# Two attentions, two feed-forwards: when scores may begin, and how far maxima run ahead

## The chip, the cores and the metric

The kernel runs on one core of a Trainium2 chip, which has eight. The metric is device time in microseconds of one execution, the median of several. Five engines take part: TensorE (PE; matmuls, and PEld, its weight loads), VectorE (DVE), ScalarE (ACT), GpSimd (POOL) and SyncE (SP), which here only issues DMAs. Each runs its own list of instructions in order and waits on semaphores for the others.

## The reference

Input x is 8 batches of 512 rows of 128 channels. Four layers follow one another, each with a residual and a layernorm behind it:

```python
x = L0_attn_x
x = _layernorm(x + _L0_attn_ref(x, Wqkv, Wproj))        # causal, rotary, 16 heads of 8
x = _layernorm(x + _L0_ffn_ref(x, ...))                  # 7 routed experts, top 2, one shared
x = _layernorm(x + _L1_attn_ref(x, Wq, Wk, Wv))          # the same without mask and projection
x = _layernorm(x + _L1_ffn_ref(x, ...))                  # gated, then three dense layers
```

The attention, which alone is changed, is

```python
Q = _apply_rope(Q, cos, sin); K = _apply_rope(K, cos, sin)
scores = einsum('bhqd,bhkd->bhqk', Q, K) / sqrt(8)
scores = where(causal, scores, finfo.min)                # layer 0 only
attn = softmax(scores)
y = einsum('bhqk,bhkd->bhqd', attn, V)
```

## The kernel before, in words

`attention` is written once and called twice, first causal (a0_), later without mask (a1_). Heads go in groups of four (HG = 4), so a batch has NG = 4 groups and all batches have 32. A group n takes PH phases: three if causal, four if not. Phase p belongs to group p // PH. A causal phase has one of three kinds: blocks of 512 columns; of 384 and 128; of 256. A batch is 12 phases (16 without mask), 96 in all (128). "Phase 5 of a batch" counts within the batch. Each phase has two halves of two heads.

Softmax needs each row's maximum, and it is taken ahead. `maxima(m, k)` computes the scores of phase m turned round, a head at a time, into one of three PSUM banks (ps_m, MB = 3); VectorE's `reduce_head` reduces each to a column of mx. When a group's maxima are known, GpSimd's `split_max` splits the negated values into two bf16 parts (L385, L387), TensorE's `turn_maxima` transposes them (L646), ScalarE copies them to mrow (L513), and SP's `max_rows` sends them by four DMAs into two more rows of qst (L325). Only then can `scores(p, half)` (L715) of that group run, which subtract the maximum in the matmul itself. ScalarE's `exp` follows (L537), GpSimd's `hide` sets the causal corner to zero (L396), and two phases later `weigh` multiplies by the values (L733).

The scores share two double banks (ps_s, SB = 2) with all other jobs of TensorE that ScalarE copies out: turn_x (L604), heads (L621), values (L628), stack (L639 and L640), turn_maxima, turn_y. They take the two banks in turn, in the order in which the planning code at the top of `attention` numbers them (S_AT). So a job waits for ScalarE's copy of the job two before it. M_AT does the same for ps_m.

A batch's way in: turn_x transposes x, heads makes q and k of all heads (copied to raw), SP's `swap_neighbours` makes a copy with pairs swapped (L333), four `rope_step`s for k and four for q rotate and split them into hi and lo (L363, L367, L373, L375; on VectorE for batch 0, on GpSimd for others), and `stack(b, i, half)` spreads them into kst (i = 0) or qst (i = 1) for the two groups of that half. Batch 0 does this ahead of the loop; batch 1's turn_x, heads and rotation stand ahead of the loop too, and later batches' are jobs at fixed phases of the loop (AT_STACK, AT_V, AT_XT, AT_HEADS, F_ROPE). The first maxima of a group with even number wait for ScalarE's copy of the stack that holds it.

LOOK is by how many phases maxima run ahead of scores: LOOK = PH + 3, so 6 if causal and 7 if not. All engines' lists are written out from the same tables; there is no scheduler.

Ahead of the loop TensorE runs:

```python
for m in range(LOOK):
    for k in range(HG):
        maxima(m, k)
    if m < 2: stack(0, m, 1)
    if m == 2: turn_x(1)
    if m == 3: heads(1)
    if m == PH: turn_maxima(0)
```

## Time and profile before

| | us |
|---|---|
| median of 3 runs | 1426.3 |
| lowest, highest | 1419.05, 1452.39 |
| the profiled execution | 1425.7 |
| its span | 1424.0 |
| TensorE busy | 1215.5 (85%) |
| VectorE, ScalarE, GpSimd busy | 849.9, 796.6, 620.8 |

The span is what the profiler saw from the first instruction to the last; the execution's own time is 1.7 us longer. The first attention lies between about 10 and 460 us of it, the second between about 684 and 1125. The granted clock in the profile's lines is a share of 2.4 GHz: 1.00 is that level, 0.50 is 1.2 GHz, and what lies between is a mixture over the stretch.

### The profile page before, as it was taken

The numbers are of one execution on the slowest core, as the hardware profiler recorded it, in microseconds if no ns is written. First come the engines' busy times: TensorE is split into PE (matmuls) and PEld (weight loads), VectorE is DVE, ScalarE is ACT, GpSimd is POOL, SyncE is SP. The second block draws the span as 40 slices with busy tenths as digits, with TensorE's granted clock in tenths as the row PEclk, the third lists the DMA queues.
The fourth block names the chain that finished last, engine by engine and source line by source line (L and its number), as shares of the span: only waits on it lengthen the run. The fifth ranks groups of instructions, "written<-read, shape, count | busy, mean of one in ns | idle before, by whom it ended". The sixth has DMA issues, their size and how long they took to land. (4 is left out here: it accounts for less than half of the span.)

```text
span 1424.0 us, 23092 instructions
## 1 busy us (share of the span) xinstructions
PE 1215.5 (85%) x8067; PEld 691.5 (49%) x8067; DVE 849.9 (60%) x2446; ACT 796.6 (56%) x1093; POOL 620.8 (44%) x790
## 2 busy tenths in 40 slices
PE   5688888888889497895589999999999779999996
PEld 2334434444444355773233444444434258888885
DVE  4466566656673467445558888888889032455443
ACT  2365556545554252543347877777878445555553
POOL 2454465655534567564133414523420325454552
PEclk8588778868776599998559999999999679999998
DMA  5000000000000000533030000000000000000000
GB/s 179 16 18 17 3 18 24 24 3 25 10 3 16 15 1 6 151 66 70 0 98 17 18 17 3 17 17 3 17 3 3 1 16 8 15 15 15 29 8 15
DMA packets 45847, 35.61 MB, mean 25 GB/s; under 512 B 5601, under 2 KB 37345, under 8 KB 45745
## 3 DMA queue, kind: packets, MB, share of 16 engines
q1 hardware_dynamic: 41760, 31.02, 6.9%
q0 software_dynamic: 3696, 2.76, 1.4%
q8 instruction: 58, 0.95, 0.3%
q10 hardware_dynamic: 288, 0.52, 0.1%
q14 instruction: 45, 0.36, 0.1%
HBM read 15.74 MB, written 8.06 MB: 17 GB/s over the span
## 5 line engine op out<-in xcount | busy, mean ns | idle before, releaser
L537 ACT ACTIVATE a_prob<-a_ps_s 128x1024 f32<-128x1024 f32 (+1 forms) x448 | 423.0, 964 | 140.3 <-PE a_ps_s L715 137.2
L807 DVE TENSOR_REDUCE a_mx<-a_ps_m 128x1 f32<-128x512 f32 x512 | 317.8, 682 | 73.5 <-PE a_ps_m L701 72.9
L701 PE MATMUL a_ps_m<-a_kst,a_qst 24*128 24x512 f32 (+3 forms) x1024 | 297.7, 498 | 19.0 <-DVE a_mx L803 11.3
L733 PE MATMUL a_ps_o<-a_prob,a_vst 128*32 128x256 f32 (+2 forms) x3328 | 302.5, 441 | 10.0 <-ACT a_oT L544 9.7
L803 DVE CUSTOM_DVE_ANT_0 a_junk<-a_ps_m,mask 128x128 f32<-128x128 f32 (+3 forms) x512 | 222.5, 486 | 130.1 <-PE a_ps_m L701 130.0
L715 PE MATMUL a_ps_s<-a_qst,a_kst 26*128 26x512 f32 (+3 forms) x1024 | 238.4, 484 | 39.8 <-ACT a_prob L537 20.6
L715 PEld LDWEIGHTS a_ps_s<-a_qst,a_kst 26*128 26x128 f32 x1024 | 100.8, 205 | 214.9 <-issue 108.7
L701 PEld LDWEIGHTS a_ps_m<-a_kst,a_qst 24*128 24x128 f32 x1024 | 137.3, 206 | 51.0 <-DVE a_mx L803 21.3
L396 POOL TENSOR_SCALAR_AFFINE_SELECT a_prob<-a_prob 128x512 f32<-128x512 f32 x128 | 79.9, 636 | 185.1 <-ACT a_prob L537 141.7
L1850 POOL TENSOR_TENSOR f_hid_lo<-f_gelu_h,f_hid_hi 128x512 fp32r<-128x512 f32 x64 | 83.1, 1298 | 101.3 <-ACT f_hid_hi L1813 101.3
L733 PEld LDWEIGHTS a_ps_o<-a_prob,a_vst 128*32 128x32 f32 x3328 | 70.9, 114 | 115.4 <-issue 99.0
L385 POOL TENSOR_SCALAR a_mpart<-a_mx 128x16 bf16<-128x16 f32 x64 | 16.5, 257 | 223.4 <-DVE a_mx L807 202.3
L1888 PE MATMUL f_ps_h<-f_hid_hi,f_h_hi 128*128 128x512 f32 x256 | 102.9, 402 | 4.0 <-POOL f_hid_lo L1850 4.0
L1890 PE MATMUL f_ps_h<-f_hid_lo,f_h_hi 128*128 128x512 f32 x256 | 101.5, 397 | 0.0
L1889 PE MATMUL f_ps_h<-f_hid_hi,f_h_lo 128*128 128x512 f32 x256 | 101.0, 395 | 0.0
L363 POOL TENSOR_TENSOR a_raw<-a_raw,rope_tables 128x1024 f32<-128x1024 f32 x28 | 66.6, 2377 | 34.2 <-DMA a_raw<-a_raw 33.1
L639 PE MATMUL a_ps_s<-a_hi,select 128*128 128x512 f32 x128 | 67.6, 528 | 12.4 <-POOL a_lo L375 6.3
L504 ACT ACTIVATE a_kst<-a_ps_s,unit 128x1024 fp32r<-128x1024 f32 x32 | 35.7, 1115 | 51.9 <-PE a_ps_s L640 51.9
L1850 POOL TENSOR_TENSOR f_hid_lo<-f_gated_h,f_hid_hi 128x512 fp32r<-128x512 f32 x32 | 41.5, 1296 | 46.7 <-ACT f_hid_hi L1802 46.0
L640 PE MATMUL a_ps_s<-a_lo,select 128*128 128x512 f32 x128 | 59.1, 462 | 0.0
L1244 ACT ACTIVATE f_gatea<-f_ps_a 128x512 f32<-128x512 f32 (+1 forms) x60 | 32.8, 547 | 44.9 <-PE f_ps_b L1338 37.3
L1888 PEld LDWEIGHTS f_ps_h<-f_hid_hi,f_h_hi 128*128 128x128 f32 x256 | 48.6, 190 | 16.2 <-POOL f_hid_lo L1850 6.5
(310 smaller groups left out, 2001.4 us busy)
## 6 DMA issues: line engine op xcount, KB each, us to landing
a_raw<-a_raw SPq DMA_DIRECT2D x28, 256.0 KB, 2.5
ef_w<-in_L_ffn_W_dram SPq DMA_DIRECT2D x21, 256.0 KB
a_qst<-a_mrow SPq DMA_DIRECT2D x256, 4.0 KB
x_tiles<-in_L_attn_x_dram SPq DMA_DIRECT2D x8, 256.0 KB, 4.6
normed_rows_dram<-ef_nrm SPq DMA_DIRECT2D x8, 256.0 KB, 2.3
f_sums<-expert_sums_dram SPq DMA_DIRECT2D x4, 512.0 KB, 5.3
f1w_h<-in_L_ffn_h_w_dram SPq DMA_DIRECT2D x2, 1024.0 KB, 6.9
f_xin<-x_tiles SPq DMA_DIRECT2D x8, 256.0 KB, 2.3
```

What stands on the lines that cost most here:

```text
L396: ins = pool.affine_select(out=diag, in_=diag, compare_op=ALU.is_ge, fill=0.0, base=0, pattern=[[0, HG], [1, P]], channel_multiplier=-1)
L537: act.activation(prob[p % RING][:, h:h + 2, 0:w], ps_s[S_AT["exp", p, u] % SB][:, :, 0:w], ACT.Exp, scale=float(D) ** -0.5).then_inc(s_tak ...
L639: pe.matmul(tile[:, v, :], select[:, i, 0, g, :], hi[:, i, :], start=True, stop=False)
L701: last = pe.matmul(tile[:, c0:c0 + w], qst[r][rows(hh, KEYS), g, P * i:P * i + P], kst[r][rows(hh, KEYS), g, 0:w], start=True, stop=True)
L715: last = pe.matmul(tile[:, v, c0:c0 + w], kst[r][rows(hh, SHIFTED), g, P * j:P * j + P], qst[r][rows(hh, SHIFTED), g, q0:q0 + w], start=Tr ...
L733: last = pe.matmul(ps_o[VW * hh:VW * hh + VW, q0:q0 + w], vst[b % 2][:, j, H // 2 * (g % 2) + HG * (g // 2) + hh, :], prob[p % RING][:, hh ...
L803: ins = dve.tensor_tensor_reduce(junk[M_AT["max", m, k] % 4][:, c0:c0 + w], tile[:, c0:c0 + w], mask[:, T - w:T], op0=ALU.add, op1=ALU.max ...
L807: ins = dve.reduce_max(mx[:, n % 2, h, i:i + 1], tile[:, c0:c0 + w], AX.X)
L1850: pool.tensor_tensor(dst, src[:, :], hi.bitcast(F32), ALU.subtract).then_inc(s_lo, 1)
L1888: pe.matmul(out, w_hi[w][:, k, cols], hi, start=start, stop=False)
L1889: pe.matmul(out, w_lo[w][:, k, cols], hi, start=False, stop=False)
L1890: return pe.matmul(out, w_hi[w][:, k, cols], lo, start=False, stop=stop)
```

## The change

Maxima ahead of the loop are cut from LOOK phases to FIRST = PH + 1. The missing ones are caught up in the loop: `known(p)` says how many phases' maxima have been issued by the end of phase p, and rises by two a phase until it reaches p + LOOK + 1. LOOK itself becomes seven if causal. Batch 0's second-half stacks move into phase 0. turn_maxima(0) now stands ahead of turn_x(1) and heads(1), and on SP max_rows(0) ahead of swap_neighbours(1). The transposes of group 1's maxima come a phase later (phase 1, or 2 without mask). Batch 1's rotation on GpSimd is dealt out over phases 0 to 3, two steps to each, behind `hide`. In every batch the next batch's first stacks move from phases 0 and 1, first half, to 3 and 4, second half; the causal second pair's q stack moves from phase 10 to 9 (without mask it stays at 12).

```diff
-    LOOK = PH + 3
+    LOOK = PH + (4 if causal else 3)
...
+    FIRST = PH + 1
...
-        AT_STACK = {(0, 0): (0, 0), (1, 0): (1, 0), (0, 1): (6, 0), (1, 1): (10, 0)}
+        AT_STACK = {(0, 0): (3, 1), (1, 0): (4, 1), (0, 1): (6, 0), (1, 1): (9, 0)}
...
-        AT_STACK = {(0, 0): (0, 0), (1, 0): (1, 0), (0, 1): (7, 0), (1, 1): (12, 0)}
+        AT_STACK = {(0, 0): (3, 1), (1, 0): (4, 1), (0, 1): (7, 0), (1, 1): (12, 0)}
...
     def turned_maxima(p):
 
+        if p in (PH - 3, PH - 2):
+            return 1 if p == PH - 2 else None
         n, now = divmod(p + 3, PH)
         return n if now == 0 and 0 < n < G else None
 
+    def known(p):
+
+        return min(PHASES, p + LOOK + 1, FIRST + 2 * (p + 1))
+
+    def maxima_at(p):
+
+        return range(known(p - 1), known(p))
...
     def stacked(p, u):
 
+        if p == 0:
+            return 0, u, 1
...
+                max_rows(0)
                 swap_neighbours(1)
-                max_rows(0)
...
                 split_max(0)
-                for i in range(2):
-                    for step in range(ROPE_STEPS):
-                        rope_step(pool, 1, i, step)
...
                     if causal and p < PHASES:
                         hide(p)
+                    if p < ROPE_STEPS:
+                        for step in (p % 2 * 2, p % 2 * 2 + 1):
+                            rope_step(pool, 1, p // 2, step)
...
-                for m in range(LOOK):
+                for m in range(FIRST):
                     for k in range(HG):
                         maxima(m, k)
-                    if m < 2:
-                        stack(0, m, 1)
-                    if m == 2:
-                        turn_x(1)
-                    if m == 3:
-                        heads(1)
-                    if m == PH:
-                        turn_maxima(0)
+                turn_maxima(0)
+                turn_x(1)
+                heads(1)
...
                         if live:
                             scores(p, half)
-                        if ahead_max:
-                            maxima(p + LOOK, 2 * half)
-                            maxima(p + LOOK, 2 * half + 1)
+                        for m in maxima_at(p):
+                            maxima(m, 2 * half)
+                            maxima(m, 2 * half + 1)
```

In the changed file the helpers' lines lie a few further on (L715 is L727, L701 is L713, L639 and L640 are L651 and L652, L646 is L658).

TensorE's list where the loop of attention 1 begins, before, from the last maxima of group 0 on. L701 is maxima, L604 turn_x, L621 heads, L646 turn_maxima, L715 scores; "x4" is the four heads.

```order
L701 MATMUL a_ps_m<-a_kst,a_qst 128x256 x4
L604 MATMUL a_ps_s<-ident,x_tiles 128x128 x4
L701 MATMUL a_ps_m<-a_kst,a_qst 128x512 x4
L621 MATMUL a_ps_s<-a_xT,heads_k 128x512
L621 MATMUL a_ps_s<-a_xT,heads_q 128x512
L646 MATMUL a_ps_s<-identb,a_mpart 32x128
L701 MATMUL a_ps_m<-a_kst,a_qst 128x128
L701 MATMUL a_ps_m<-a_kst,a_qst 128x384
```

Three more such pairs, four blocks of 256 and then L715 follow. The same place in the changed kernel:

```order
L713 MATMUL a_ps_m<-a_kst,a_qst 128x256 x4
L713 MATMUL a_ps_m<-a_kst,a_qst 128x512 x4
L658 MATMUL a_ps_s<-identb,a_mpart 32x128
L616 MATMUL a_ps_s<-ident,x_tiles 128x128 x4
L633 MATMUL a_ps_s<-a_xT,heads_k 128x512
L633 MATMUL a_ps_s<-a_xT,heads_q 128x512
L727 MATMUL a_ps_s<-a_qst,a_kst 128x512 x2
L713 MATMUL a_ps_m<-a_kst,a_qst 128x128
```

The transpose of the maxima stands ahead of turn_x and heads, and the scores follow the heads at once, with the maxima of phase 4 behind them.

TensorE's list in the changed kernel from the second half of phase 4 into phase 5 of the first batch, with its waits: a0_taken counts ScalarE's copies, a0_mtaken VectorE's, a0_rope1 the rotation of q. L651 and L652 are the q stack, L727 scores, L713 maxima of the next batch.

```order
L713 MATMUL a_ps_m<-a_kst,a_qst 128x256 [waits a0_mtaken] x2
L651 MATMUL a_ps_s<-a_hi,select 128x512 [waits a0_rope1,a0_taken]
L652 MATMUL a_ps_s<-a_lo,select 128x512
L651 MATMUL a_ps_s<-a_hi,select 128x512
L652 MATMUL a_ps_s<-a_lo,select 128x512
L727 MATMUL a_ps_s<-a_qst,a_kst 128x256 [waits a0_taken]
L727 MATMUL a_ps_s<-a_qst,a_kst 128x256
L713 MATMUL a_ps_m<-a_kst,a_qst 128x512 [waits a0_taken,a0_mtaken]
L713 MATMUL a_ps_m<-a_kst,a_qst 128x512 [waits a0_mtaken]
```

Before, nothing stood between phase 4's last maxima and phase 5's first scores, and phase 5 held the previous kind of maxima, still of the same batch. Now the stack stands there, and the first L713 behind it waits for ScalarE's copy of that very stack.

GpSimd's list at the start of attention 1, before: the split of group 0 (L385, L387), then all eight steps of batch 1's rotation, group 1's split, and only then `hide` (L396).

```order
L387 TENSOR_TENSOR a_mpart<-a_mx,a_mpart 128x4x4
L363 TENSOR_TENSOR a_raw<-a_raw,rope_tables 128x1024
L367 TENSOR_TENSOR a_rope<-a_raw 128x512
L373 CAST a_hi<-a_rope 128x512
L375 TENSOR_TENSOR a_lo<-a_rope,a_hi 128x512
...
L385 TENSOR_SCALAR a_mpart<-a_mx 128x4x4
L387 TENSOR_TENSOR a_mpart<-a_mx,a_mpart 128x4x4
L396 AFFINE_SELECT a_prob<-a_prob 128x4x128 x4
```

In the changed kernel:

```order
L400 TENSOR_TENSOR a_mpart<-a_mx,a_mpart 128x4x4
L409 AFFINE_SELECT a_prob<-a_prob 128x4x128
L376 TENSOR_TENSOR a_raw<-a_raw,rope_tables 128x1024
L380 TENSOR_TENSOR a_rope<-a_raw 128x512
L398 TENSOR_SCALAR a_mpart<-a_mx 128x4x4
L400 TENSOR_TENSOR a_mpart<-a_mx,a_mpart 128x4x4
L409 AFFINE_SELECT a_prob<-a_prob 128x4x128 x2
L386 CAST a_hi<-a_rope 128x512
L388 TENSOR_TENSOR a_lo<-a_rope,a_hi 128x512
```

The first `hide` and group 1's split no longer stand behind the whole rotation.

## Rows read from the trace of the kernel before

**Rows 1.** The page, busy time, share of the span and instructions of each engine.

```profile
PE 1215.5 (85%) x8067; PEld 691.5 (49%) x8067; DVE 849.9 (60%) x2446; ACT 796.6 (56%) x1093; POOL 620.8 (44%) x790
```

**Rows 2.** Windows: stretch, length, busy (count) of PE, PEld, DVE, ACT, POOL, clock.

```profile
26.05:70.12 44.07, 31.58 (x115) 16.41 (x116) 20.61 (x95) 11.80 (x16) 13.69 (x15) 0.50 0.08 26
698.74:742.47 43.73, 34.83 (x103) 16.57 (x104) 24.34 (x40) 13.85 (x17) 11.88 (x12) 0.50 0.26 79
70.00:460.00 390.00, 336.81 (x2634) 161.22 (x2634) 240.74 (x1110) 219.03 (x301) 200.94 (x330) 0.78 0.04 14
900.00:1000.00 100.00, 94.64 (x860) 40.90 (x857) 84.91 (x158) 79.13 (x94) 38.61 (x54) 1.00 0.04 15
```

**Rows 3.** Timeline, start of attention 1: start, duration, engine, line, tiles [idle before, releaser].

```profile
41.78 1.92 PE L621 MATMUL a_ps_s<-a_xT,heads_q 128*128 128x512 f32 x2
...
44.74 0.25 ACT L513 ACTIVATE a_mrow<-a_ps_s 32x128 f32<-32x128 bf16 x1
...
46.41 2.80 SPq L325 DMA_DIRECT2D a_qst<-a_mrow  x4
...
50.47 0.79 PE L715 MATMUL a_ps_s<-a_qst,a_kst 26*128 26x512 f32 x2 [1.86 <-DMA a_qst<-a_mrow]
```

**Rows 4.** Timeline, start of attention 1: reductions, a stack's matmul, a stack's copy.

```profile
28.11 0.69 DVE L803 CUSTOM_DVE_ANT_0 a_junk<-a_ps_m,mask 128x512 f32<-128x512 f32 x1
...
28.94 0.63 PE L640 MATMUL a_ps_s<-a_lo,select 128*128 128x512 f32 x1
...
30.46 1.11 ACT L504 ACTIVATE a_kst<-a_ps_s,unit 128x1024 fp32r<-128x1024 f32 x1 [4.47 <-PE a_ps_s L640]
...
31.51 0.55 DVE L803 CUSTOM_DVE_ANT_0 a_junk<-a_ps_m,mask 128x384 f32<-128x384 f32 x1
...
35.92 0.42 DVE L803 CUSTOM_DVE_ANT_0 a_junk<-a_ps_m,mask 128x256 f32<-128x256 f32 x1
```

**Rows 5.** Timeline, start of attention 2.

```profile
699.57 2.48 DVE L807 TENSOR_REDUCE a_mx<-a_ps_m 128x1 f32<-128x512 f32 x4 [4.13 <-PE a_ps_m L701]
...
719.59 1.28 ACT L537 ACT_TABLE_LOAD   x1
719.66 2.69 SPq L325 DMA_DIRECT2D a_qst<-a_mrow  x4
...
723.61 0.80 PE L715 MATMUL a_ps_s<-a_qst,a_kst 26*128 26x512 f32 x2
```

**Rows 6.** Timeline, attention 1, phases 0 and 1: TensorE behind GpSimd.

```profile
54.14 0.76 PE L639 MATMUL a_ps_s<-a_hi,select 128*128 128x512 f32 x1 [2.75 <-POOL a_lo L375]
...
60.48 0.27 PE L646 MATMUL a_ps_s<-identb,a_mpart 128*32 128x128 bf16 x1 [3.57 <-POOL a_mpart L387]
```

**Rows 7.** Two windows in the loop of attention 1, columns as in rows 2.

```profile
124.00:134.00 10.00, 8.43 (x87) 4.53 (x89) 6.19 (x26) 6.88 (x10) 6.05 (x8) 1.00 0.15 55
186.00:196.00 10.00, 9.12 (x64) 3.66 (x64) 8.82 (x47) 4.65 (x6) 5.31 (x8) 0.50 0.01 2
```

**Rows 8.** Waits of TensorE, 70 to 460: total us, times, longest.

```profile
PE a_ps_s L646 <- POOL a_mpart L387: 13.9, 10, 2.7
PE a_ps_m L701 <- DVE a_mx L803: 7.5, 9, 1.1
PE a_ps_s L715 <- ACT a_qst L506: 7.0, 13, 0.6
PE a_ps_s L715 <- ACT a_raw L485: 4.2, 6, 0.7
```

**Rows 9.** Windows: phase 9 at full and low clock, phases 10 and 11.

```profile
93.79:96.63 2.84, 2.70 (x26) 0.96 (x26) 2.70 (x10) 2.09 (x3) 2.25 (x3) 1.00 0.00 0
96.63:102.17 5.54, 4.92 (x52) 2.49 (x52) 4.78 (x25) 4.28 (x6) 3.03 (x4) 1.00 0.02 6
140.81:144.89 4.08, 3.63 (x26) 1.13 (x26) 3.11 (x10) 2.10 (x3) 1.61 (x3) 0.50 0.00 0
```

**Rows 10.** Timeline, phase 6 of the third batch: the transpose of maxima.

```profile
184.63 0.22 PE L646 MATMUL a_ps_s<-identb,a_mpart 128*32 128x128 bf16 x1 [1.67 <-POOL a_mpart L387]
```

More of the change, by code:

```diff
@@ L212, in m_slot @@
         M_AT[key] = len(M_AT)
-    for b in range(2):
-        s_slot("xT", b)
-        for i in range(2 if b == 0 else 1):
-            s_slot("heads", b, i)
-        if b == 0:
-            s_slot("v", 0)
-            for half in range(2):
-                for i in range(2):
-                    s_slot("stack", 0, i, half)
+    s_slot("xT", 0)
+    for i in range(2):
+        s_slot("heads", 0, i)
+    s_slot("v", 0)
+    for i in range(2):
+        s_slot("stack", 0, i, 0)
     s_slot("mT", 0)
-    for m in range(LOOK):
+    s_slot("xT", 1)
+    s_slot("heads", 1, 0)
+    for m in range(FIRST):
         for k in range(HG):
@@ L241, in attention @@
             s_slot("mT", turned_maxima(p))
-        for k in range(HG):
-            if p + LOOK < PHASES:
-                m_slot("max", p + LOOK, k)
+        for u in range(2):
+            for m in maxima_at(p):
+                for k in (2 * u, 2 * u + 1):
+                    m_slot("max", m, k)
         for name, k in (("norm", pair_at(p, NORM_AT)),
@@ L438, in _ @@
                 split_max(0)
-                for i in range(2):
-                    for step in range(ROPE_STEPS):
-                        rope_step(pool, 1, i, step)
                 for p in range(LAST + 2 * PH if front is None else FINAL):
@@ L549, in _ @@
                 values(0)
-                for half in range(2):
-                    for i in range(2):
-                        stack(0, i, half)
+                for i in range(2):
+                    stack(0, i, 0)
+                turn_maxima(0)
                 turn_x(1)
                 heads(1)
-                turn_maxima(0)
                 if front is not None:
@@ L744, in _ @@
                 stack(0, 1, 0)
-                for m in range(LOOK):
+                for m in range(FIRST):
                     for k in range(HG):
                         maxima(m, k)
-                    if m < 2:
-                        stack(0, m, 1)
-                    if m == 2:
-                        turn_x(1)
-                    if m == 3:
-                        heads(1)
-                    if m == PH:
-                        turn_maxima(0)
+                turn_maxima(0)
+                turn_x(1)
+                heads(1)
                 for p in range(FINAL):
@@ L758, in _ @@
                     old = p - LAG if 0 <= p - LAG < PHASES else None
-                    ahead_max = p + LOOK < PHASES
                     for half in range(2):
@@ L762, in _ @@
                             scores(p, half)
-                        if ahead_max:
-                            maxima(p + LOOK, 2 * half)
-                            maxima(p + LOOK, 2 * half + 1)
+                        for m in maxima_at(p):
+                            maxima(m, 2 * half)
+                            maxima(m, 2 * half + 1)
                         if old is not None:
@@ L848, in _ @@
                         rope_step(dve, 0, i, step)
-                for m in range(LOOK):
+                for m in range(FIRST):
                     for k in range(HG):
@@ L853, in _ @@
                     for half in range(2):
-                        if p + LOOK < PHASES:
-                            reduce_head(p + LOOK, 2 * half)
-                            reduce_head(p + LOOK, 2 * half + 1)
+                        for m in maxima_at(p):
+                            reduce_head(m, 2 * half)
+                            reduce_head(m, 2 * half + 1)
                         if batch_at(p, F_LN, -1) is not None:
```

## The prediction

> **What bounds the kernel now.** I read the busy times and the clock line first, then stretches (windows) of the two attentions, then who waited for whom, then the timeline of both starts. TensorE is busy 85% of the span [rows 1], so its own order is what counts. But the stages differ. The second attention runs at granted clock 1.00 (2.4 GHz) with TensorE busy 94.64 of 100 us; the first loop, 390 us long, has it busy 336.81 us at a mean clock of 0.78 [rows 2], so (1 - 0.78)/0.5 = 44% of that loop, some 170 us, runs at the lower level, 1.2 GHz. Both starts are poor: from the first maxima to phase 3 TensorE is busy 31.58 of 44.07 us in attention 1 (26.05 to 70.12), and in attention 2 34.83 of 43.73 us (698.74 to 742.47), both at 0.50 [rows 2]. At the starts the chain of maxima, their split on GpSimd, a transpose, a 4 us DMA and only then the first scores is the bound; after that GpSimd's rotation of batch 1, for which TensorE's stack waits.
>
> **Attention 1, start.** Before: six phases of maxima, stacks and batch 1's heads stand ahead of scores(0), which start at 50.47 [rows 3]. Now four phases. VectorE paces maxima: one 512-wide tile every 0.61 us, a 128+384 pair of reductions 0.69, a 256-wide tile 0.35 [rows 4]. From 26.88: phase 0 takes 2.5 us, phase 1 2.8, phase 2 1.4, so group 0 is known at 33.6 (before 36.95). GpSimd's split, two short instructions (before: 37.29 to 37.87), is done at 34.6. TensorE's last matmul of phase 3 starts when a bank is freed, about 34.4, so the transpose comes at 34.9, its copy (0.25 [rows 3]) ends at 35.5. SP now sends these four DMAs ahead of the swap, which cost 1.4 us of waiting before (copy ended 44.99, DMA began 46.41). From issue to scores passed 4.06 us once and 3.95 us the other time [rows 3, 5]: data at 39.5. Meanwhile TensorE turns x and waits for its copy, about 2 us, and makes the heads, two pairs of 1.92 [rows 3]: end 40.7. Thus scores(0) at 40.7, **9.8 us sooner**, and the heads, not the DMA, come last.
>
> That lead is partly paid back. Phases 0 to 2 now hold seven phases of maxima where three stood, and the two stacks of batch 0's other half. Without any rise of the clock: phase 0 is scores 1.5, maxima about 3.0, two stacks of 2.4 us (0.80 + 3 x 0.63 [rows 4]), about 9.5 us in all; phase 1, eight tiles for VectorE (2.46 + 2.76) plus 0.4 us until the stack's copy lets group 2's maxima begin, 6.6 us; phase 2, maxima, weigh and values, 8 us. Phase 3 then starts at 64.7, not 70.12 [rows 2]: 5.5 us sooner. But batch 1's two stacks (2 x 2.4) have moved behind it and one phase of maxima (1.8) ahead of it: 5.5 - 4.8 + 1.8 = 2.5 us. If the clock rises at once when the heads end, TensorE's pieces shrink (a stack 1.3 to 1.5, values 1.05), VectorE becomes the bound, and phase 3 comes at about 60: 10.3 - 3.0 + 0.95 = 8.3 us. Before, it rose at 69 to 70, after TensorE had worked nearly without a gap from 60.7; now it has such a stretch from 36.9 to about 48. I take **6 us**, nearer the upper end. What TensorE waited on GpSimd there (2.75 and 3.57 us [rows 6]) goes, since the rotation's steps now come two to a phase and stack (1,0,0) is asked for in phase 3 only.
>
> **Attention 2, start.** Same way. VectorE starts at 699.57, 0.62 us a tile: group 0 known at 709.5, transpose at 710.6 behind five phases, DMA at 711.3, data 715.3; x and heads end at 716.3. Scores(0) at 716.3 for 723.61 [rows 5]. The load of ScalarE's table (1.28 us [rows 5]), which was hidden in a wait, now stands between the heads' copy and the first exp; it ends at 718.7, while TensorE needs that bank at 720.4 at the earliest, so I cost it at nothing. At the low clock phase 3 starts at 740 for 742.47 [rows 2]: 2.5 us, less the stacks that are still to come (3.0): -0.5. With a clock that rises by 718: 734.3, so 8.2 - 3.0 = 5.2. I take **4 us**; 3.6 us of waits for the rotation go, and the dense stretch is as long as in attention 1. The weights' DMAs behind max_rows(0) only move up.
>
> **The loop of attention 1.** Three edits act in each of 7 later batches.
> (a) Maxima run seven phases ahead, so kinds are paired anew. VectorE's maxima per phase were 2.46, 2.76, 1.4 us [rows 4] beside TensorE's 2.84 and, for the next two kinds, 5.54 with a stack of 1.3 in it, so about 2.1 each [rows 9]. They are now 2.76, 1.4, 2.46, while TensorE's share shifts by 0.2 at most: no kind has VectorE over TensorE by more than 0.2, where it was 0.6. The layernorm's moments still fall into phases 7 and 8. TensorE's wait for VectorE in this loop is 7.5 us in 9 places [rows 8]; I take half, **-4**. Ends: 0, and -7.5.
> (b) Stack (·,0,0) in phase 3's second half is followed at once by the transpose of maxima, and with two banks the scores of phase 4 need the stack's bank: its copy takes 1.11 us [rows 4], less the 0.22 of the transpose, about 1.0. Stack (·,1,0) in phase 4's second half waits for the heads' copy, 0.4 us, and the maxima of phase 5 are now those of the next batch, which may begin only when this copy is done: 1.02 + 0.1 less 0.3 of scores, about 0.9. Queued behind these maxima are weigh, turn_y, all of TensorE; VectorE idles as well. 7 x 2.3 = **+16**.
> (c) Gone are the waits at the old places: scores on the q stack's copy 7.0 us in 13, on the heads' copy 4.2 in 6 [rows 8]: 11.2; of the pair moved from phase 10 to 9, about 0.3 each, 2 us, come back at the transpose. Net **-9**. GpSimd's lateness at the transpose, 13.9 us in 10 places [rows 8], stays: the rotation step of 2.38 us ahead of the split in phase 6 (TensorE idle 1.67 us ahead of 184.63 [rows 10]) is not moved.
> Loop: -4 + 16 - 9 = **+3 us**. Attention 2's loop has four phases to a group and banks free in time, and LOOK is unchanged: 0, cover being that its maxima for the next batch come in phase 9, four phases behind the stacks. Phases at the end with no maxima are one more for one less elsewhere: 0.
>
> **Sum.** -6 - 4 + 3 = -7 against the profiled execution's 1425.7 (span 1424.0), which lies 0.6 below the median 1426.3. Forecast **1419 us**.
>
> **The clock, and the page.** What I hold constant is the 170 us at the lower clock. The rows: in phases 3 to 5 it is at 1.00 (124 to 134) though TensorE idles 0.7 and 0.87 us there, but after the wait of 1.67 us that ends at 184.63 [rows 10] it falls, and 186 to 196 is all at 0.50 [rows 7]. The Trainium skill, page "TensorE: Matmul & The Clock Gate", section "A second HAM failure mode: psum-queue depth-cycling", says that a kernel cycling through banks can idle briefly between groups of matmuls often enough that the clock oscillates. By that rule the three new waits in phases 3 to 5, 2.3 us together, would cost the full clock there; the trace agrees so far that single waits under 0.9 us leave it and 1.67 us did not.
>
> **Rivals.**
> 1. *The waits pull the clock down in each batch (slower side).* Phases 3 to 5 then run at the low level, and, as phases 0 and 1 have lost their stacks, dense work that let it rise comes later. A phase costs 4.08 us at the low level and 2.84 at the full [rows 9], 1.24 more. With three phases more at the low level per batch 7 x 3 x 1.24 = 26: 1419 + 26 = **1445**, and with four, and the starts' gain at its lower end, past 1454. It decides once more than one phase a batch is lost (8.7 us, more than the gain). For: dense stretches move; against: stacks and heads close together are 5 us of matmuls without a gap.
> 2. *The new pairing and the lost waits keep the clock up.* The drop in phase 2 follows 0.62 us on the q stack's copy and 0.86 on another; the first is gone. With 2.5 fewer low phases a batch: 7 x 2.5 x 1.24 = 22: **1397**. Against: phase 6's drop, the longest, has its cause left in place.
> 3. *The starts give nothing.* The clock rises no sooner, both starts at their lower ends (2.5 - 0.5), loop +3, hence **1426**: scores begin early but only trade places with maxima.
>
> **Numbers.** Forecast 0.48 (its own range 1408 to 1429), rival 1 0.22, rival 2 0.17, rival 3 0.13. The range takes in two of three parts of rivals 1 and 2: **1394 to 1442**. About 2% (28 us) is what a measurement tells from no change here. Faster by that means under 1397.8: most of rival 2 and a tail, 0.17. Slower means over 1454.8: a quarter of rival 1, 0.07. Within: 0.76.
>
> **What would show it.** First scores near 40.7 and 716.3 (DMA ahead of the swap, heads' matmuls ending just before); granted clock at 1.00 before 55 and before 730, or else 0.50 to 60 (rival 3); no wait of a stack on the rotation at the starts. In the loop: waits of scores on the k stack's copy and of maxima on the q stack's, some 7 each of 0.9 us, the old 13 gone; wait on GpSimd's split still near 14 us; mean clock near 0.78. A mean below 0.74 is rival 1, above 0.82 rival 2. The forecast is wrong if the clock's share moves by more than a tenth, whatever the waits do.

## The result: slower by 1.2%, at a lower clock

| us | before | after |
|---|---|---|
| median of 20 runs each, same chip | 1434.34 | 1442.55 |
| ratio, 95% interval | | 1.0117 [1.0079, 1.0155] |
| profiled execution, its span | 1425.7, 1424.0 | 1446.9, 1445.2 |
| mean granted clock of the span | 0.859 | 0.834 |

The ratio leaves out executions more than 1.5% above the fastest of their kernel (13 of the 20 before, 5 of the 20 after), which the medians don't: by the ratio the change is some 17 us slower, by the medians 8.2. Either way it is slower where 7 us faster was forecast: the wrong sign, and the median just outside the range. Stages of the two profiled executions:

| us | before | after | change |
|---|---|---|---|
| attention 1, first maxima to first scores | 24.42 | 14.95 | -9.5 |
| its batch 0 (first scores to batch 1's) | 51.7 | 67.6 | +15.9 |
| its batches 1 to 6 | 314.0 | 328.6 | +14.6 |
| its batch 7, to the last scores | 43.0 | 46.0 | +3.1 |
| attention 2, first maxima to last scores | 426.4 | 423.35 | -3.1 |
| all else | 564.5 | 564.6 | +0.1 |

The first attention lost 24 us. (The two profiled executions lie 21 us apart, more than the medians or the ratio say of the kernels.) The page of after, for [rows 1]:

```profile
PE 1259.2 (87%) x8067; PEld 715.2 (49%) x8067; DVE 848.6 (59%) x2446; ACT 796.9 (55%) x1093; POOL 622.1 (43%) x790
```

The same 8067 matmuls took 43.7 us more; the other engines' busy times moved by at most 1.3. Windows of after, for [rows 2], same columns; the fourth is batches 1 to 6:

```profile
26.89:70.96 44.07, 39.95 (x145) 22.23 (x146) 25.81 (x120) 12.45 (x17) 13.37 (x17) 0.50 0.09 29
70.00:460.00 390.00, 346.75 (x2465) 167.17 (x2468) 229.66 (x1064) 206.00 (x283) 193.83 (x312) 0.72 0.04 14
722.93:766.66 43.73, 40.36 (x141) 19.43 (x142) 28.26 (x46) 16.81 (x20) 11.98 (x12) 0.58 0.27 79
109.44:438.08 328.64, 291.46 (x2108) 143.11 (x2104) 196.93 (x915) 175.38 (x242) 165.27 (x269) 0.74 0.04 14
```

and of before, batches 1 to 6:

```profile
102.17:416.17 314.00, 269.25 (x2110) 130.26 (x2106) 197.22 (x915) 175.48 (x242) 165.94 (x270) 0.79 0.04 14
```

In 390 us of the loop TensorE is 10 us busier and got through 169 matmuls fewer: 0.72 where it was 0.78. In batches 1 to 6 it idles less than before (37.2 us for 44.8) and takes 14.6 us longer. Time multiplied by clock hardly differs (unrounded, 242.8 for 247.4). It is not short of work, it does the work slower.

The first scores came as worked out. Timeline of after at both, for [rows 3, 5]:

```profile
40.00 1.91 PE L633 MATMUL a_ps_s<-a_xT,heads_q 128*128 128x512 f32 x2
41.84 0.79 PE L727 MATMUL a_ps_s<-a_qst,a_kst 26*128 26x512 f32 x2
```

```profile
739.60 1.06 PE L633 MATMUL a_ps_s<-a_xT,heads_q 128*128 128x512 f32 x1
740.59 0.79 PE L727 MATMUL a_ps_s<-a_qst,a_kst 26*128 26x512 f32 x2
```

First scores follow the first maxima by 14.95 us (forecast 14.65, before 24.42) and 17.66 (forecast 17.6, before 24.87), right behind the heads. TensorE's waits in after, 70 to 460, for [rows 8]:

```profile
PE a_ps_s L727 <- ACT a_prob L550: 8.6, 20, 0.7
PE a_ps_s L727 <- ACT a_kst L517: 7.2, 7, 1.0
PE a_ps_m L713 <- ACT a_qst L519: 6.2, 7, 0.9
PE a_ps_s L651 <- ACT a_raw L498: 4.6, 6, 0.8
PE a_ps_s L658 <- POOL a_mpart L400: 4.0, 3, 1.8
PE a_ps_m L713 <- DVE a_mx L809: 2.2, 5, 0.5
```

The new waits are there, seven each of 1.0 and 0.9 us as foretold, the heads' at 0.8 where 0.4 was forecast. Waits for VectorE fell from 7.5 to 2.2, for GpSimd from 13.9 to 4.0. All of TensorE's idling in these 390 us is 43.3 us, before 53.2; so it is not the waits' own length that costs. One place, batch 4, phases 4 to 6, timeline and then windows of after:

```profile
291.69 0.23 PE L658 MATMUL a_ps_s<-identb,a_mpart 128*32 128x128 bf16 x1
292.96 0.44 PE L727 MATMUL a_ps_s<-a_qst,a_kst 26*128 26x384 f32 x2 [1.04 <-ACT a_kst L517]
...
297.14 0.50 PE L651 MATMUL a_ps_s<-a_hi,select 128*128 128x512 f32 x1 [0.77 <-ACT a_raw L498]
...
299.54 0.79 PE L713 MATMUL a_ps_m<-a_kst,a_qst 24*128 24x512 f32 x2 [0.89 <-ACT a_qst L519]
300.27 1.08 PE L745 MATMUL a_ps_o<-a_prob,a_vst 128*32 128x256 f32 x8
...
306.35 0.80 PE L651 MATMUL a_ps_s<-a_hi,select 128*128 128x512 f32 x1
306.94 0.63 PE L652 MATMUL a_ps_s<-a_lo,select 128*128 128x512 f32 x1
...
309.87 2.08 PE L681 MATMUL a_ps_m<-wproj,a_yT 128*128 128x128 f32 x8
```

```profile
294.00:296.50 2.50, 2.38 (x14) 0.94 (x10) 0.36 (x3) 1.03 (x2) 0.00 (x0) 1.00 0.02 7
296.50:299.50 3.00, 1.51 (x6) 0.86 (x6) 0.74 (x4) 2.63 (x4) 1.33 (x3) 0.95 0.63 214
299.50:319.50 20.00, 19.57 (x115) 9.44 (x115) 11.35 (x50) 8.94 (x13) 8.57 (x11) 0.50 0.03 10
319.50:323.00 3.50, 3.50 (x36) 1.75 (x28) 3.33 (x19) 1.16 (x3) 3.23 (x3) 0.98 0.00 0
```

The clock falls at 299.2, within the third of three waits in 8 us, and stays at 1.2 GHz for 20 us although TensorE is busy 19.57 of them. Some 7 of these are matmuls over the whole array (128 rows and 128 columns): the second pair's stack, whose first two matmuls are shown, the projection and two transposes. I read the clock of the whole loop in windows of half a microsecond. At this wait for the q stack's copy or within 3 us behind it the clock falls in five of eight batches (0, 1, 3, 4 and 5); in batch 2 the same three waits of 1.04, 0.76 and 0.89 us pass at the full clock. In batches 1 to 6 it falls 13 times and is low for 171.6 us, 13.2 a fall; before, 18 times and 133.1 us, 7.4 a fall. Fewer falls, each longer.

### The profile page after: what moved, and what is told of

The parts are those of the page before. It is cut to its first block and busy times, and to the rows that moved or that the text cites. A ratio compares the mean times of both kernels' runs of the same rounds, so it can differ in the third digit from the quotient of the medians.

```text
span 1445.2 us, 23092 instructions
## 1 busy us (share of the span) xinstructions
PE 1259.2 (87%) x8067; PEld 715.2 (49%) x8067; DVE 848.6 (59%) x2446; ACT 796.9 (55%) x1093; POOL 622.1 (43%) x790
## 5 line engine op out<-in xcount | busy, mean ns | idle before, releaser
L813 DVE TENSOR_REDUCE a_mx<-a_ps_m 128x1 f32<-128x512 f32 x512 | 316.8, 683 | 67.8 <-PE a_ps_m L713 67.7
L713 PE MATMUL a_ps_m<-a_kst,a_qst 24*128 24x512 f32 (+3 forms) x1024 | 315.6, 519 | 16.7 <-ACT a_qst L519 9.4
L745 PE MATMUL a_ps_o<-a_prob,a_vst 128*32 128x256 f32 (+2 forms) x3328 | 316.7, 460 | 10.6 <-ACT a_oT L557 8.5
L727 PE MATMUL a_ps_s<-a_qst,a_kst 26*128 26x512 f32 (+3 forms) x1024 | 245.7, 503 | 30.8 <-ACT a_prob L550 19.5
L727 PEld LDWEIGHTS a_ps_s<-a_qst,a_kst 26*128 26x128 f32 x1024 | 104.5, 215 | 214.9 <-issue 117.2
L713 PEld LDWEIGHTS a_ps_m<-a_kst,a_qst 24*128 24x128 f32 x1024 | 149.3, 218 | 49.4 <-DVE a_mx L809 16.4
L376 POOL TENSOR_TENSOR a_raw<-a_raw,rope_tables 128x1024 f32<-128x1024 f32 x28 | 66.6, 2379 | 26.0 <-DMA a_raw<-a_raw 26.0
L651 PE MATMUL a_ps_s<-a_hi,select 128*128 128x512 f32 x128 | 63.9, 499 | 12.0 <-DVE a_lo L388 6.1
L652 PE MATMUL a_ps_s<-a_lo,select 128*128 128x512 f32 x128 | 55.7, 435 | 0.0
```

The costliest lines, as they stand in the source:

```text
L376: eng.tensor_tensor(raw[:, i, :, :], raw[:, i, :, :], tables[:, :, :], ALU.mult).then_inc(s_rope[i], 1)
L713: last = pe.matmul(tile[:, c0:c0 + w], qst[r][rows(hh, KEYS), g, P * i:P * i + P], kst[r][rows(hh, KEYS), g, 0:w], start=True, stop=True)
L727: last = pe.matmul(tile[:, v, c0:c0 + w], kst[r][rows(hh, SHIFTED), g, P * j:P * j + P], qst[r][rows(hh, SHIFTED), g, q0:q0 + w], start=Tr ...
L745: last = pe.matmul(ps_o[VW * hh:VW * hh + VW, q0:q0 + w], vst[b % 2][:, j, H // 2 * (g % 2) + HG * (g // 2) + hh, :], prob[p % RING][:, hh ...
L813: ins = dve.reduce_max(mx[:, n % 2, h, i:i + 1], tile[:, c0:c0 + w], AX.X)
```

## The experiments

The first expectations name theories. A: the loss is in the places of the stacks, whose full-array work used to lift the clock in phases 0 and 1. B: it is in LOOK 7. C: only the new waits' own time. "Batches 1 to 6" is attention 1's 72 phases in one profiled execution, after 328.6 us at 0.739, before 314.0 at 0.788.

**LOOK and the places, apart.**

```diff
 e1: after; the causal stacks of batches 2 to 7 at the old phases, LOOK 7
+        LATER_STACK = {(0, 0): (0, 0), (1, 0): (1, 0), (0, 1): (6, 0), (1, 1): (9, 0)}
 e2: after
-    LOOK = PH + (4 if causal else 3)
+    LOOK = PH + 3
 e3: before
-        AT_STACK = {(0, 0): (0, 0), (1, 0): (1, 0), (0, 1): (6, 0), (1, 1): (10, 0)}
+        AT_STACK = {(0, 0): (3, 1), (1, 0): (4, 1), (0, 1): (6, 0), (1, 1): (9, 0)}
 e5: e1 with LOOK = PH + 3 and (1, 1): (10, 0), the starts alone
 e6: before
-    LOOK = PH + 3
+    LOOK = PH + (4 if causal else 3)
```

> The changed kernel, but from batch 2 on the causal attention's first stacks stand again in phases 0 and 1, first half (batch 1's stay in 3 and 4; the q stack of the second pair stays in phase 9; LOOK stays 7). Theory A (the loss comes from where the stacks stand: phases 0 and 1 have lost their dense matmuls, so TensorE's clock stays at the lower level there, and three new waits of 1.0, 0.8 and 0.9 us stand in phases 3 to 5): the time falls below before, ratio 0.985 to 1.000, the mean clock of 110 to 430 us returns from 0.71 to 0.78 or more, and attention 1 from its first maxima to its last scores, 433 us before and 457 changed, takes 425 to 435. Theory B (LOOK of 7 pairs the kinds of maxima badly): the ratio stays at 1.01, the clock at 0.72 and attention 1 over 450. Theory C (only the new waits' own 2.7 us a batch count, not the clock): it takes 438 to 442.

> The changed kernel with LOOK = 6 in the causal attention; stacks as changed. The next batch's maxima then begin in phase 6, so the 0.9 us wait on the q stack's copy in phase 5 goes. Theory A: most of the loss stays, ratio 1.00 to 1.01, attention 1 at 447 to 455, clock in phases 0 to 3 still low. Theory B: the loss goes, attention 1 at 425 to 435, ratio under 1.00.

> The kernel before with the changed causal table of stacks alone: (3, second half), (4, second half), (6), (9). All else as before, LOOK 6. Theory A: slower than before by 15 to 30 us, ratio 1.010 to 1.020, and waits of scores on the k stack's copy near 7 us in 7 or 8. Theory B: within 0.3% of before. Theory C: 8 to 12 us slower.

> The changed kernel with LOOK at six again and, from batch 2 on, the stacks at their old phases: both starts are the change's, the causal loop is that of before. If the loss lies in LOOK 7 (theory B), the first attention's batches 1 to 6 take 312 to 316 us at a mean clock of 0.78 to 0.79 as before (314.0, 0.788), batch 0 about 73 us, the starts keep what they give (9 us in attention 1, 3 us in attention 2), and the kernel is at 0.991 to 0.998 of before. If the starts themselves cost the later loop its clock (a rival that no kernel so far excludes), batches 1 to 6 go above 318 us and the ratio is over 1.000.

> The kernel before with LOOK at seven and nothing else changed. Theory B (LOOK 7 takes the clock down, wherever the stacks stand): batches 1 to 6 of attention 1 take 326 to 331 us at 0.72 to 0.74, and the kernel is at 1.007 to 1.014 of before. Theory A (the loss is in the places of the stacks, or in the two together): batches 1 to 6 stay at 312 to 318 us and the ratio is 0.997 to 1.003.

| | LOOK | first pair's stacks | ratio to before | batch 0 | batches 1 to 6, clock |
|---|---|---|---|---|---|
| e1 | 7 | old | 1.0058 [1.0015, 1.0101] | 67.6 | 328.8, 0.724 |
| e2 | 6 | new | 1.0014 [0.9979, 1.0049] | 58.0 | 314.1, 0.771 |
| e3 | 6 | new | 1.0041 [1.0009, 1.0073] | 56.5 | 316.6, 0.754 |
| e5 | 6 | old | no interval | 58.2 | 318.3, 0.762 |
| e6 | 7 | old | 1.0027 [0.9981, 1.0074] | 54.3 | 309.8, 0.787 |

Of e5, one execution (1394.08) lies 22 us below all others, so no ratio was formed; its median is 1428.1 beside 1424.35. Theory A falls as the main cause: e2 has the new places and is at par with before. But e3, the new places with the old starts, is slower by 0.4%, some 6 us, with an interval that leaves out 1: the places cost something, and e2's starts cover it. Theory C falls: the waits of scores on the k stack are in e2 too (6.2 us in 6 places between 100 and 430). LOOK 7 it is, with the new places (e2 to after, +14.5 us in batches 1 to 6) and in e1's profile with the old (+10.5 on e5's); but e6's profile, 309.8, is of an execution of 1417.8 beside a median of 1433.7 (before 1424.35), and e1's of one of 1448.1 beside 1431.4: with the old places seven takes one course or the other, and one profile doesn't tell its mean.

Where e2 and after differ can be read phase by phase. Of the 14.5 us, phases 5 and 6 take 17.8 more (65.8 for 48.0), all others 3.3 less. The time at the low clock in batches 1 to 6 is 143.5 us in e2 and 171.6 in after, and all of the 28 us more stand in phases 3 to 8 (24.4 and 66.2; the rest 119.1 and 105.4). Work that takes 28 us at 1.2 GHz takes 14 at 2.4: by this estimate the clock alone is as much as the difference.

And e5 contradicts my expectation: starts alone don't give 9 + 3 us. In batch 0 they hand back 6.5 of the first 9.5 (58.2 for 51.7).

**Distance or pairing.**

```diff
 e8: before; e9: before
-    LOOK = PH + 3
+    LOOK = PH + (5 if causal else 3)     # e8, q stack (1, 1) at (9, 0)
+    LOOK = PH + (6 if causal else 3)     # e9, q stack (1, 1) at (8, 1), mx four deep
```

> The kernel before with LOOK at eight (the second pair's q stack a phase earlier, as it must be). A phase then meets maxima of a third kind: 512 columns of scores beside two heads' of 256, and so on. If the distance ahead is what costs (maxima run further ahead, more waits of their stacks), batches 1 to 6 lose again at least the 14 us that seven cost; if it is the pairing of kinds, eight is a pairing of its own and may lie on either side of six: then over 3 us from seven. No change from six (312 to 316 us) says that seven's pairing alone is bad.

> The kernel before with LOOK at nine: a phase meets maxima of its own kind again, as with six, but three phases further ahead (mx four deep, the second pair's q stack at phase 8, second half). If the pairing of kinds is what costs in seven and eight, nine gives back what six has: 312 to 318 us in batches 1 to 6 and within 0.4% of before. If the distance ahead is what costs, nine is at least as slow as eight: over 335 us in batches 1 to 6, 1.015 or more of before.

Eight: 1.0202 [1.0153, 1.0250], batches 1 to 6 at 337.8 us and 0.742. Nine: 1.0051 [1.0000, 1.0102], 320.8 us, 0.771, median of all 1425.7 beside 1428.9. Neither meets its expectation in full: nine lies above the 0.4% and the 318 us of the pairing's case and far below the 335 us of the distance's. So distance alone is not what costs. That the pairing is, as six and nine beside eight suggest, isn't shown: seven with the old places and starts (e6) is at 1.0027, and eight and nine also move the second pair's q stack. VectorE's relief, for which I had put down a gain, came with seven and with a loss.

**Can matmuls that only add work buy the clock back?**

```diff
 e4: after, scores of phases 0 and 1 three and two times over (26 rows of the array)
+                    again = (3, 2)[u] if causal and p >= BATCH and p % BATCH < 2 else 1
 e7: e2, ahead of each half's scores in phases 0 and 1, four of
+                                pe.matmul(tile[:, v, :], select[:, 0, 0, 0, :], kst[r][:, g, :], start=True, stop=True)
 e10: e2, the same number, place and columns over 26 rows
+                                pe.matmul(tile[:, v, :], kst[r][rows(hh, SHIFTED), g, 0:P], kst[r][rows(hh, SHIFTED), g, :],
 e11: after with e7's lines.  e12: e7 in phase 0 alone
```

> The changed kernel; in phases 0 and 1 of batches 1 to 7 of the causal attention the scores' matmuls are issued 3 times in the first half and 2 times in the second, into the same bank with the same result: about 1.3 us more of TensorE's work a phase at the full clock, in place of the stack that left. Theory A in its strong form (what phases 0 and 1 lack is dense work, and the clock follows it): the clock in phases 1 to 3 rises from 0.5 towards 1.0, and though 14 phases of 1.3 us (18 us) are added, attention 1 grows by less than 8 us or shrinks. If the clock does not hang on it: 18 to 28 us slower than changed, attention 1 at 475 to 485.

> The changed kernel with LOOK 6, and four more matmuls over all 128 rows, 512 columns each, written into the scores' bank ahead of each half's scores in phases 0 and 1 of batches 1 to 7 (their result is overwritten, they only add work): 16 a batch, 112 in all. If the clock falls in phases 0 to 2 because the full-array work of the stacks is gone from there (theory A), the clock of phases 0 to 2 rises from 0.50 to 0.56 to over 0.65, and batches 1 to 6 take less than the filler's own time more: under 323 us against 314.1. If the level is set by the waits and not by how full the array is, phases 0 to 2 stay at 0.5 to 0.6 and the filler costs its own time at the low level, 16 x 0.43 us = 7 us a batch, some 40 us in batches 1 to 6.

> The kernel with the dense filler again (the changed kernel with LOOK 6 and sixteen more matmuls of 512 columns a batch, in phases 0 and 1 of batches 1 to 7), but over 26 rows of the array where that one has 128. Same number, same places, same columns. If a busy TensorE is what keeps the clock, phases 0 to 10 are again at 0.95 or more and batches 1 to 6 take 315 to 320 us. If the rows count, phases 0 to 2 stay at 0.50 to 0.60, the filler costs its time at the low level, 0.43 us each, and batches 1 to 6 take 335 to 355 us, the kernel 1.015 to 1.03 of before.

> The changed kernel, LOOK 7, with the dense filler of 112 matmuls. If its loss against LOOK 6 is the granted clock alone, the filler takes it back: batches 1 to 6 at a clock of 0.85 or more and 312 to 325 us, against 328.6 without, and the kernel within 0.5% of the LOOK 6 kernel with the same filler (1430.1), so 1.002 to 1.010 of before and under the changed kernel's own 1.0117. If LOOK 7 costs something of its own (waits that a full clock doesn't shorten), batches 1 to 6 stay over 328 us.

> The LOOK 6 kernel with half of the dense filler: the eight matmuls of phase 0 of each batch, none in phase 1 (56 in all). The full filler adds 96 x 0.213 = 20.5 us of work in batches 1 to 6 and costs 2.7 us, so it gives back about 18. If the clock stays up once it has risen in phase 0, half of the filler keeps most of that: batches 1 to 6 take 304 to 312 us, and the kernel is at 0.992 to 0.999 of before. If phases 1 and 2 fall back to 0.5, it is 316 to 322 us and 1.001 to 1.006.

| | ratio to before | batches 1 to 6, clock | phases 0, 1, 2, clock |
|---|---|---|---|
| e4 | 1.0194 [1.0134, 1.0253] | 337.1, 0.743 | 0.65, 0.55, 0.53 |
| e7 | 1.0060 [1.0028, 1.0092] | 316.8, 0.883 | 0.85, 1.00, 1.00 |
| e10 | 1.0186 [1.0101, 1.0271] | 335.2, 0.740 | 0.50, 0.50, 0.56 |
| e11 | 1.0261 [1.0148, 1.0373] | 335.6, 0.826 | 0.87, 0.95, 0.74 |
| e12 | 0.9957 [0.9895, 1.0019] | 321.4, 0.829 | 0.87, 1.00, 0.63 |

Batches 1 to 6, first e7, then e10, in windows:

```profile
100.73:417.57 316.84, 275.93 (x2201) 138.64 (x2200) 197.15 (x914) 175.73 (x242) 163.90 (x269) 0.88 0.04 14
```

```profile
103.57:438.79 335.22, 298.53 (x2202) 151.07 (x2200) 197.42 (x914) 175.75 (x242) 164.86 (x270) 0.74 0.04 13
```

Same number of matmuls, places and columns. Over 128 rows they lift phases 0 to 2 to 0.85, 1.00 and 1.00 (e2: 0.50, 0.50, 0.55) and cost 2.7 us for some 22 us of added work (96 matmuls, whose starts lie 0.23 us apart at the full clock in e7); over 26 rows they lift nothing and cost 21 us. Here a busy TensorE alone does not raise the clock; what raised it had full rows (and other data: e7's weights are those of the stack, e10's are k). e4 is undecided: its repeated scores of 26 rows leave phases 0 to 2 where after has them (0.58, 0.56, 0.53) but for 0.07 in phase 0, as if they didn't help, while by the ratios it is 11 us slower than after, less than the 18 to 28 foretold for that case.

Full rows by themselves are no guarantee either: in the 20 low microseconds of after above, four stack matmuls of 512 columns in a row and eight of the projection left the clock at 0.50. Why that stretch is so long is open. e11 refutes what I expected of it: with the filler the clock of after's batches 1 to 6 rises from 0.739 to 0.826, with phases 3 to 7 at 1.00, and still they take 7.0 us more than without; it is low in 2 and in 8 to 10 (0.74; 0.73, 0.70, 0.74, where e7 has 1.00; 0.76, 0.95, 0.93). Half the filler neither wins nor loses: e12's interval spans 1, and its median of all is 1433.1 beside 1428.9.

**The wait behind the q stack, taken from LOOK 7 and given to LOOK 6.**

```diff
 e13: after, causal
-        AT_STACK = {(0, 0): (3, 1), (1, 0): (4, 1), (0, 1): (6, 0), (1, 1): (9, 0)}
+        AT_STACK = {(0, 0): (2, 1), (1, 0): (3, 1), (0, 1): (6, 0), (1, 1): (9, 0)}
 e14: e2, causal
+        AT_STACK = {(0, 0): (4, 1), (1, 0): (5, 1), (0, 1): (6, 0), (1, 1): (9, 0)}
 e15: after, unaltered.  e16: before, unaltered
```

> The changed kernel, LOOK 7 kept, with the causal first pair's stacks a phase earlier: phases 2 and 3, second half. ScalarE's copy of the q stack then has a phase's time before the next batch's first maxima at phase 5, so their new wait of 0.89 us goes. If that wait is what pulls the clock down in the changed kernel (in five of eight batches the clock falls within 3 us behind it), phases 5 and 6 rise from 0.78 and 0.74 to over 0.9, batches 1 to 6 take 310 to 320 us against 328.6, and the kernel is at 0.998 to 1.006 of before. If LOOK 7's loss is in the mix of work, batches 1 to 6 stay over 325 us and the ratio at 1.010 or more.

> The LOOK 6 kernel with the causal first pair's stacks a phase later, 4 and 5, second half, so that it gets the wait that the changed kernel has: the next batch's first maxima, at phase 6 here, stand right behind the q stack and wait some 0.9 us for its copy. If this wait pulls the clock down, phase 6 and 7 fall from 1.00 to below 0.85, batches 1 to 6 take 320 to 332 us against 314.1, and the kernel is at 1.006 to 1.014 of before. If it costs its own time alone, it is 6 x 0.9 = 5 us: 317 to 320 us and 1.002 to 1.006.

> The changed kernel unaltered, for a second look at where its clock falls. If its falls are tied to places in the program, they stand behind the same waits as in the first look (the q stack's copy ahead of phase 5's maxima, the copied weights ahead of phase 10's scores) and batches 1 to 6 take 324 to 332 us at 0.73 to 0.75. If they are chance, they stand elsewhere and the total may be anything from 310 to 335.

> The kernel before unaltered, for a second look at the same. Tied to the program: batches 1 to 6 again at 310 to 318 us and 0.78 to 0.80, falls behind GpSimd's split of the maxima in phase 7 and VectorE's reduction in phase 8. Chance: over 320 or under 308 us.

| | ratio to before | batch 0 | batches 1 to 6, clock | phases 5, 6, clock |
|---|---|---|---|---|
| e13 | 1.0003 [0.9956, 1.0049] | 70.3 | 309.7, 0.770 | 0.88, 0.92 |
| e14 | 1.0020 [0.9991, 1.0048] | 57.5 | 317.1, 0.769 | 1.00, 1.00 |
| e15, after | 1.0151 [1.0078, 1.0223] | 65.1 | 331.4, 0.721 | 0.69, 0.66 |
| e16, before | 0.9986 [0.9945, 1.0028] | 51.5 | 308.7, 0.807 | 0.92, 0.90 |

The second profile of after falls at or behind the q stack in six of eight batches. From 244 us on all its eight falls stand within 0.1 us of the first profile's, three of them behind the q stack: the falls belong to the program. e13 has no such wait, its batches 1 to 6 take 19 us less than in after's first profile, 22 less than in its second, and of their low time 18.7 us stand in phases 3 to 8 where after has 66.2 and 75.2 (the rest 123.8 for 105.4 and 109.4). So the loss hangs on where the stacks stand with LOOK 7. That the wait for the q stack is the trigger fits this, but isn't shown alone: e13 also moves the stacks' own work a phase ahead, and its clock still falls in phase 5 in three of eight batches (0, 5 and 6). Of all executions of e13 the median is 1430.2 beside 1425.0: most of the loss is regained, not surely all. Timeline of e13, same phases of the same batch, and its window:

```profile
284.97 0.23 PE L658 MATMUL a_ps_s<-identb,a_mpart 128*32 128x128 bf16 x1
286.15 0.45 PE L727 MATMUL a_ps_s<-a_qst,a_kst 26*128 26x384 f32 x2 [0.95 <-ACT a_qst L519]
...
290.33 0.38 PE L727 MATMUL a_ps_s<-a_qst,a_kst 26*128 26x256 f32 x2 [0.76 <-ACT a_raw L498]
290.44 0.49 PE L713 MATMUL a_ps_m<-a_kst,a_qst 24*128 24x512 f32 x2
```

```profile
284.50:291.00 6.50, 4.79 (x36) 2.05 (x38) 2.17 (x13) 4.06 (x6) 2.23 (x3) 1.00 0.15 43
```

Two waits of 0.95 and 0.76, 4 us apart, pass at full clock, 1.71 us of idling in 6.5. One batch later the same two don't; e13, timeline and windows:

```profile
340.32 0.45 PE L727 MATMUL a_ps_s<-a_qst,a_kst 26*128 26x384 f32 x2 [0.95 <-ACT a_qst L519]
...
344.50 0.38 PE L727 MATMUL a_ps_s<-a_qst,a_kst 26*128 26x256 f32 x2 [0.76 <-ACT a_raw L498]
```

```profile
340.00:346.00 6.00, 4.92 (x40) 2.29 (x40) 2.45 (x11) 3.87 (x6) 1.66 (x3) 1.00 0.20 59
347.00:353.00 6.00, 6.00 (x40) 2.59 (x32) 2.63 (x13) 2.37 (x3) 4.76 (x6) 0.50 0.05 19
```

The same waits in the same program can pass or bring a fall, so no length or distance of waits that decides it can be read from these runs. In e14 the wait for the q stack has only a short one on either side (0.31 us, ending 3.9 us ahead, and 0.41). It passes at the full clock in all of batches 1 to 6 and costs its own time, no more:

```profile
285.22 0.50 PE L713 MATMUL a_ps_m<-a_kst,a_qst 24*128 24x512 f32 x2 [0.77 <-ACT a_qst L519]
...
288.83 0.23 PE L658 MATMUL a_ps_s<-identb,a_mpart 128*32 128x128 bf16 x1 [0.41 <-ACT a_kst L517]
```

```profile
282.00:290.00 8.00, 6.82 (x54) 3.59 (x53) 3.40 (x12) 5.19 (x7) 4.33 (x6) 1.00 0.01 5
```

So this wait alone does not bring the fall. In after it ends 2.4 us behind another of 0.77; that this company is what makes the difference is argued, not shown. LOOK 6 has a place with falls too, in phase 8: e2's clock falls there in six of eight batches, behind

```profile
236.29 0.38 PE L713 MATMUL a_ps_m<-a_kst,a_qst 24*128 24x256 f32 x1 [1.08 <-DVE a_mx L809]
```

which LOOK 7 cuts to 0.5 us and less, as I had reckoned, and which was cheap where it stood: in e2 phases 8 and 9 at 0.73 and 0.79, 0.95 again in 10, against 0.78 and 0.74 in phases 5 and 6 of after and on into 8.

Of the expectations for e15 and e16, the places of the falls came true for e15; its clock (0.721) and both of e16's figures lie a little outside.

**Both pieces together.**

```diff
 e17: e13 from batch 1 on; ahead of that e2's stacks, and maxima six ahead until phase 9
+        look = LOOK - 1 if causal and p < 9 else LOOK
+        return min(PHASES, p + look + 1, FIRST + 2 * (p + 1))
```

> What the runs so far point to: the changed kernel with the causal first pair's stacks at 2 and 3, second half, from batch 2 on (no wait behind the q stack, 309.7 us for batches 1 to 6), but batch 0 as in the LOOK 6 kernel: its stacks at 3 and 4, and maxima six phases ahead until phase 9, seven from there. LOOK 7 cost batch 0 ten to twelve microseconds (70.3 us from first scores to batch 1's with the stacks earlier, 58.0 with LOOK 6), part of it a wait of 3.89 us for GpSimd's rotation. If both add up, batch 0 takes 56 to 61 us, batches 1 to 6 stay at 308 to 316 us, and the kernel is at 0.990 to 0.997 of before. If the clock's later course gives the start back, as in the kernel with the starts alone, the ratio is 0.997 to 1.004.

1.0013 [0.9972, 1.0054], medians of all 1423.96 and 1428.27. Batches 1 to 6 repeat at 309.8 us, 0.770; attention 1 from first maxima to last scores takes 431.5 us (before 433.1 and, in e16, 430.4; after 457.2). But batch 0 takes 66.4, not 56 to 61; 3.7 of the 8.4 us over e2's stand in a phase 9 of 9.05 us at 0.50 (e2: 5.35 at 0.81). The best version found is level with before, not faster.

## Why the prediction was wrong

- **Attention 1, start, -6:** mechanism and times of the first scores right (9.5 us sooner), size wrong. I had reckoned with the clock rising before 55; it stayed at 0.50 through all of 26.89 to 70.96, and phase 3 began at 64.8, where the sum without a rise had put it (64.7). Batch 0, 51.7 and 51.5 us in the two profiles of before, takes 58.0 to 63.4 in the five profiles whose kernels share e2's batch 0 (mean 60.3) and 63.0 to 69.6 in the five that share after's (mean 66.6). So of the 9.5 us LOOK 6 hands back some 9, and LOOK 7 some 15: net about -1 and +5.5.
- **Attention 2, start, -4:** scores 7.2 us sooner, and the lead holds: from first maxima to the scores of the last batch pass 370.8 to 372.1 us in the thirteen profiles with the new start, 380.2 to 381.9 in the six with the old. The last batch gives it back: 51.2 to 51.8 us in all thirteen, 38.3, 38.4, 38.4, 45.9, 51.6 and 51.6 in the six, by the clock there. The whole attention takes 418.6 to 433.6 us with the old start (mean 424.9) and 422.2 to 423.7 with the new. A gain of some 2 us is in reach of these, nothing more.
- **Loop (b), new waits, +16, and (c), -9:** number as forecast, length too but for the heads' (0.8 us for 0.4); the three kinds add up to 18.0 us. Their own time was not what they cost.
- **Loop (a), VectorE's relief, -4:** VectorE's waits went (7.5 to 2.2 us), and GpSimd's, which I had left in place (13.9 to 4.0). That is some 15 us of waits saved, and the loop still became slower.
- **The step that failed: "What I hold constant is the 170 us at the lower clock".** The sum put the clock's part at nothing. Between 70 and 460 the low time was 175 us before and 219 after (mean clock 0.78 and 0.72), in batches 1 to 6 133.1 and 171.6. The clock is a result of where waits and work stand. The ground for holding it constant, that single waits under 0.9 us leave it, did not carry over to waits that follow one another, and the trace of before already showed it: behind two of 0.72 and 0.62, 3.4 us apart, the clock falls at 202.9.

```profile
197.67 0.44 PE L715 MATMUL a_ps_s<-a_qst,a_kst 26*128 26x384 f32 x2 [0.72 <-ACT a_prob L537]
...
201.05 0.39 PE L715 MATMUL a_ps_s<-a_qst,a_kst 26*128 26x256 f32 x2 [0.62 <-ACT a_qst L506]
```

```profile
197.00:202.50 5.50, 4.21 (x44) 2.31 (x44) 4.44 (x23) 4.22 (x6) 4.22 (x9) 1.00 0.02 4
203.00:206.00 3.00, 3.00 (x21) 0.91 (x14) 1.72 (x8) 1.22 (x2) 2.91 (x5) 0.50 0.02 5
```

A mean clock of 0.72 in 70 to 460 is what I had set down as rival 1, with 1445 us and a chance of 0.22; the profiled execution took 1446.9. That the number fits so well is luck: the rival has +29 us in the loop and keeps the starts' -10, while batches 1 to 7 lost 17.7 and the starts with batch 0 came to +3.3. One half of its mechanism held: phases 3 to 5, at the full clock in e2 but for 0.94 in phase 3, fell to 0.81, 0.94 and 0.78. The other half, that phases 0 and 1 without their stacks cost time, did not: e2 has these phases at 0.50 throughout, and its batches 1 to 6 take what before's take. By the rule of the Trainium skill, page "TensorE: Matmul & The Clock Gate", section "A second HAM failure mode: psum-queue depth-cycling", brief idling between groups of matmuls makes the clock oscillate; the trace agrees, with the addition that the same two waits, 4 us apart, pass in batch 4 of e13 and bring a fall in batch 5. My argument against the rival, that stacks and heads together are 5 us of dense matmuls, did not hold: at 299.2 the clock falls with heads and stack right ahead of the wait.

How much of the loss the clock carried can be weighed without any profile. Each execution comes with its span and mean clock, and over the 29 of before that ran beside e1 to e4 the span falls by 9.4 us for each 0.01 of clock; over the 20 of after by 11.2. Their means are 1422.2 us at 0.8555 and 1440.9 at 0.8359: 0.0196 of clock is 18 to 22 us, and the difference is 18.7. (The two sets ran on different chips; the ratio above is the fair one.) This fits, and proves nothing alone: by the same slopes e2, at a mean of 0.8483, should lie 7 to 8 us over before and lies 0.5 over.

**Open.** Why LOOK 7 costs batch 0 some 6 us more, which e17 didn't get rid of; a part is that after issues one phase of maxima more by the end of phase 2 (ten for nine), and phase 3 starts 22.95 us behind the first scores where it starts 19.6 behind them with LOOK 6 (means of the same five and five profiles). Which of the moved wait and the moved work keeps e13's clock up. What makes seven with the old places go either way (e1, e6). Why eight is slow: its clock is as low, but no change of one wait was tried on it.

## What to carry to other kernels

A wait on a TensorE that is busy 85% of the time is priced by whether the clock falls behind it and how long it stays low, not by its length: 0.8 us cost half a microsecond a batch in one place (e14 on e2: 2.9 us in six), while moving the stacks so that a wait of 0.9 us went gave back over 3 in another (after's two profiles to e13: 18.9 and 21.7 us in six). So before work is moved, list where the clock falls and rises in the trace, and look at what the move puts ahead of a fall and takes away behind it. One profile is one draw: where a kernel's executions range over 3%, a stage's time wants a second profile, or the span and clock of every run.
